# Attention block on one core: sequence-wide two-bank score tiles, fillers in a new order, middle casts on ScalarE

## The reference

```python
B, R, K, M = (16, 64, 128, 128); H, D = (8, 16); FF = 512
q = (route @ wq + bq).reshape(b_, r_, k_, H, D)      # k and v alike
scores = jnp.einsum('brkhd,brnhd->brknh', q, k) / D ** 0.5
attn = jax.nn.softmax(scores, axis=3)
out = jnp.einsum('brknh,brnhd->brkhd', attn, v).reshape(b_, r_, k_, m_)
x = _layernorm(route + (out @ wo + bo), ln1_g, ln1_b)
ff = jax.nn.relu(x @ w1 + b1) @ w2 + b2
return _layernorm(x + ff, ln2_g, ln2_b)
```

## Time and profile before

| | |
|---|---|
| median of three runs | 4756.37 us |
| the profiled execution | 4760.15 us, span 4758.1 us |
| TensorE matmul busy | 4435.0 us, 93% of the span |
| VectorE busy | 3915.0 us, 82% |
| GpSimd busy | 3623.5 us, 76% |
| ScalarE busy | 3391.7 us, 71% |
| DMA engines busy | 42.4% for the kernel's own queue |
| granted TensorE clock | 0.994 of 2.4 GHz on average |

### The profile page before, as it was taken

The page is one execution under the profiler, slowest core; times in us unless marked ns, Lnnn a source line. Parts: engine busy times, 40 slices in busy tenths (PEclk is TensorE's granted clock), DMA queues, the critical chain, the costliest instruction groups (busy, mean ns, idle before and its releaser), DMA issues.

```text
span 4758.1 us, 159188 instructions
## 1 busy us (share of the span) xinstructions
PE 4435.0 (93%) x51984; PEld 3739.4 (79%) x51984; DVE 3915.0 (82%) x11275; ACT 3391.7 (71%) x6401; POOL 3623.5 (76%) x4620
## 2 busy tenths in 40 slices
PE   5999999999999999999999999999999999999998
PEld 4787878877878877878878778878787878787886
DVE  5888888878888888888888878888888888888886
ACT  2777777767777776777777767777776777777776
POOL 4777777777777777777777777777777777777776
PEclk9999999999999999999999999999999999999999
DMA  4444444444444444444444444444444444444441
GB/s 116 115 121 119 120 120 117 122 113 119 119 120 116 122 115 122 114 121 116 123 116 121 119 116 116 123 116 121 119 121 110 123 116 121 119 121 116 120 121 53
DMA packets 756319, 556.46 MB, mean 117 GB/s; under 512 B 95872, under 2 KB 755328, under 8 KB 755456
## 3 DMA queue, kind: packets, MB, share of 16 engines
q1 hardware_dynamic: 755456, 545.81, 42.4%
HBM read 69.47 MB, written 67.11 MB: 29 GB/s over the span
## 4 chain that ended last, share of the span: by engine, by line
PE 51%; DVE 27%; issue 11%; ACT 7%; SPq 1%; DVEq 1%; ACTq 0%; POOL 0%; DMA 0%; POOLq 0%
PE bankC L629 10%; PE bankB L629 9%; DVE max_sb L535 7%; PE bankA L745 6%; PE oT_ps L645 6%; PE s_ps L662 5%; PE sT_ps L676 4%; DVE st L494 4%; PE bankB L607 4%; DVE xT_parts L559 4%; DVE ob_sb L466 4%; ACT parts L362 4%; PE bankC L601 3%; DVE onT_sb L479 3%; ACT xT_parts L407 3%
## 5 line engine op out<-in xcount | busy, mean ns | idle before, releaser
L379 ACT ACTIVATE prob_sb<-sT_ps 128x512 f32<-128x512 f32 x2048 | 1222.7, 597 | 1067.5 <-PE sT_ps L676 1067.3
L535 DVE TENSOR_REDUCE max_sb<-s_ps 128x4 f32<-128x512 f32 x2048 | 1367.6, 668 | 7.3 <-PE s_ps L662 6.1
L266 POOL TENSOR_TENSOR parts<-rest_sb,parts 128x512 bf16<-128x512 f32 x512 | 595.8, 1164 | 503.7 <-DVE parts L459 503.7
L662 PE MATMUL s_ps<-stack 96*128 96x128 bf16 x8192 | 811.7, 222 | 20.5 <-issue 14.2
L676 PE MATMUL sT_ps<-stack 99*128 99x128 bf16 x8192 | 796.9, 219 | 3.7 <-DMA stack<-max_parts 3.6
L662 PEld LDWEIGHTS s_ps<-stack 96*128 96x128 bf16 x8192 | 531.8, 98 | 339.2 <-issue 317.6
L645 PE MATMUL oT_ps<-prob_sb,v_ones 128*32 128x128 f32 x16384 | 555.1, 276 | 0.0
L676 PEld LDWEIGHTS sT_ps<-stack 99*128 99x128 bf16 x8192 | 547.8, 97 | 5.6 <-DMA stack<-max_parts 4.0
L466 DVE STREAM_TRANSPOSE ob_sb<-oT_ps 128x512 f32<-128x512 f32 x512 | 364.5, 712 | 203.5 <-PE oT_ps L645 192.7
L645 PEld LDWEIGHTS oT_ps<-prob_sb,v_ones 128*32 128x32 f32 x16384 | 417.2, 110 | 123.3 <-issue 90.6
L629 PE MATMUL bankC<-w_sb,h_sb 128*128 128x128 f32 x4096 | 513.0, 278 | 0.0
(11 more groups left out here) (80 smaller groups left out, 9256.1 us busy)
## 6 DMA issues: line engine op xcount, KB each, us to landing
stack<-parts SPq DMA_DIRECT2D x3072, 128.0 KB, 2.5
x_sb<-in_x SPq DMA_DIRECT2D x256, 256.0 KB, 3.1
out<-out_sb SPq DMA_DIRECT2D x256, 256.0 KB, 3.3
stack<-max_parts SPq DMA_DIRECT2D x768, 8.0 KB, 1.9
w_sb<-in_L_conv_w SPq DMA_DIRECT2D x2, 256.0 KB, 3.1
be_row<-in_L_conv_ln_b SPq DMA_DIRECT2D x2, 256.0 KB, 20.4
g_row<-in_L_conv_ln_g SPq DMA_DIRECT2D x2, 256.0 KB, 23.7
bo_row<-in_L_conv_bo SPq DMA_DIRECT2D x1, 256.0 KB, 8.9
```

The source lines that it names most:

```text
L266: pool.tensor_tensor(parts[:, r % 2, 3 * c + LO], rest_sb[:, c], parts[:, r % 2, 3 * c + MID], ALU.subtract).then_inc(lo_split, 1)
L379: act.activation(prob_sb[:, n % 4], sT_ps[n % 2][:], ACT.Exp, scale=float(D) ** -0.5).then_inc(exp_done, 1)
L535: dve.reduce_max(max_sb[:, (r - 2) % 2, half * HU:(half + 1) * HU, s], s_ps[n % 2][:].rearrange("p (h k) -> p h k", h=HU), AX.X).then_inc( ...
L662: ins = pe.matmul(s_ps[n % 2][:, j * P:(j + 1) * P], stack[0:PROD, (r - 2) % 4, 0, h, tok], stack[0:PROD, (r - 2) % 4, 1, h, tok], start=T ...
```

## The change

1. A step has four slots w instead of eight units. A slot scores one sequence's eight heads into one two-bank tile `s_ps` (128x1024), and the same for `sT_ps`. There is one tile of each, so a slot's scores wait for the maximum of the slot before, and its turned scores for the exponential of the slot before. VectorE takes one maximum and ScalarE one exponential of 128x1024 per slot. `prob_sb` is two buffers of eight heads (same bytes as before).
2. The fillers are in a new order. Slot 0: wo for group r-5 (it was r-4, at the end of the step), hidden chunks 2 and 3 of r-6, the transposes of x. Slot 1: both halves of `down` in a row, `attend`. Slot 2: transposes of the first norm's output, the query and the key projection. Slot 3: the transpose of the maxima (now group r-2, into `oT_ps`, not A), hidden chunks 0 and 1 of r-5, the value projection (now group r, not r-1), `attend`. The last slot scores the first sequence of group r-1, one step earlier than before.
3. The two middle casts move from VectorE to ScalarE (`mid_part`), after the last exponential of the step.
4. SyncE's order in a step is: store, load of x, the three maximum rows (of group r-2), and the 12 stack DMAs, six for the queries and then six for the keys, where each six waits for its own low part only.
5. The second normalisation is applied in two halves, one at the end of a step and one in the next; its statistics are taken in two halves beside `add_y`. ScalarE and GpSimd get one step more at the end of the program.

The diff, cut to its core:

```diff
-        s_ps = [ctx.enter_context(nc.psum_tensor(f"s_ps{b}", [P, T], F32)) for b in range(2)]
-        sT_ps = [ctx.enter_context(nc.psum_tensor(f"sT_ps{b}", [P, T], F32)) for b in range(2)]
+        s_ps, sT_ps = (ctx.enter_context(nc.psum_tensor(n, [P, H * P], F32)) for n in ("s_ps", "sT_ps"))
...
-        def sT_unit(u):
-            return (4, u + 4) if u < 4 else (3, u - 4)
+        def scored(w):
+            return (1, 0) if w == 3 else (2, w + 1)
+        def attended(w):
+            return (4, w + 2) if w < 2 else (3, w - 2)
... SyncE
+                if live(t, r, 2):
+                    sp.wait_ge(max_parts_made, upto(t, r, 2, plus=1))
+                    for part in range(MAXROWS):
+                        sp.dma_start(stack[PROD + part:PROD + part + 1, (r - 2) % 4, 0],
+                                     max_parts[:, part]).then_inc(max_rows_loaded, DMA)
                 if live(t, r, 0):
-                    sp.wait_ge(lo_split, upto(t, r, 0, per=2, plus=2))
-                    for j in range(len(Q_PARTS)):
-                        for c, part in enumerate((Q_PARTS[j], K_PARTS[j])):
+                    for c, order in enumerate((Q_PARTS, K_PARTS)):
+                        sp.wait_ge(lo_split, upto(t, r, 0, per=2, plus=c + 1))
+                        for j, part in enumerate(order):
... ScalarE
+            def mid_part(t, r, c):
+                act.wait_ge(rest_made, upto(t, r, 0, per=2, plus=c + 1))
+                act.activation(parts[:, r % 2, 3 * c + MID], rest_sb[:, c], ACT.Copy).then_inc(mid_split, 1)
...
+            def exponentials(t, r, w):
+                lag, s = attended(w)
+                if live(t, r, lag):
+                    act.wait_ge(sT_done, upto(t, r, lag, per=SEQS, plus=s + 1))
+                    if (v := upto(t, r, lag, per=2, plus=s // 2)) is not None:
+                        act.wait_ge(pv_done, v)
+                    act.activation(prob_sb[:, s % 2], sT_ps[:], ACT.Exp, scale=float(D) ** -0.5).then_inc(exp_done, 1)
... VectorE
+            def row_max(t, r, w):
+                lag, s = scored(w)
+                if live(t, r, lag):
+                    dve.wait_ge(s_done, upto(t, r, lag, per=SEQS, plus=s + 1))
+                    if (v := upto(t, r, lag, plus=-1)) is not None:
+                        dve.wait_ge(maxT_done, v)
+                    dve.reduce_max(max_sb[:, (r - lag) % 2, :, s], s_ps[:].rearrange("p (h k) -> p h k", h=H),
+                                   AX.X).then_inc(max_done, 1)
... TensorE
+            def scores(t, r, w):
+                lag, s = scored(w)
+                if live(t, r, lag):
+                    tok = slice(s * P, (s + 1) * P)
+                    if s == 0:
+                        pe.wait_ge(stack_loaded[(r - lag) % 2], upto_dma(t, r, lag, per=STACK_DMAS * DMA))
+                    if (v := upto(t, r, lag, per=SEQS, plus=s)) is not None:
+                        pe.wait_ge(max_done, v)
+                    for h in range(H):
+                        ins = pe.matmul(s_ps[:, h * P:(h + 1) * P], stack[0:PROD, (r - lag) % 4, 0, h, tok],
+                                        stack[0:PROD, (r - lag) % 4, 1, h, tok], start=True, stop=True)
+                    ins.then_inc(s_done, 1)
```

More of the change, by code:

```diff
@@ L216, in step @@
             def step(t, r):
[L218 to L222, removed]
+                if live(t, r, 7):
+                    sp.wait_ge(out_ready, upto(t, r, 7, plus=1))
+                    sp.dma_start(out_g[t + (r - 7)], out_sb[:, (r - 7) % 2]).then_inc(out_stored[(r - 7) % 2], DMA)
                 if live(t, r, -1):
@@ new lines, in scores_turned @@
+            def scores_turned(t, r, w):
+                lag, s = attended(w)
+                if live(t, r, lag):
+                    tok = slice(s * P, (s + 1) * P)
+                    if s == 0:
+                        pe.wait_ge(max_rows_loaded, upto(t, r, lag, per=MAXROWS * DMA, plus=MAXROWS * DMA))
+                    if (v := upto(t, r, lag, per=SEQS, plus=s)) is not None:
+                        pe.wait_ge(exp_done, v)
+                    for h in range(H):
+                        ins = pe.matmul(sT_ps[:, h * P:(h + 1) * P], stack[:, (r - lag) % 4, 1, h, tok],
+                                        stack[:, (r - lag) % 4, 0, h, tok], start=True, stop=True)
+                    ins.then_inc(sT_done, 1)
@@ new lines, in attend @@
+            def attend(t, r, lag, half):
+                pe.wait_ge(exp_done, upto(t, r, lag, per=SEQS, plus=2 * half + 2))
+                pe.wait_ge(v_copied, upto(t, r, lag, plus=1))
+                if (v := upto(t, r, lag, per=2, plus=half)) is not None:
+                    pe.wait_ge(oT_turned, v)
+                for k in range(2):
+                    for h in range(H):
+                        j, f = h % HU, h // HU
+                        ins = pe.matmul(oT_ps[j * VW:(j + 1) * VW, (2 * k + f) * P:(2 * k + f + 1) * P],
+                                        v_ones[:, (r - lag) % 4, 2 * half + k, h], prob_sb[:, k, h * P:(h + 1) * P],
@@ new lines, in step @@
+                scores(t, r, 0)
+                scores_turned(t, r, 0)
+                if live(t, r, 5):
+                    pe.wait_ge(onT_made, upto(t, r, 5, plus=1))
+                    pe.wait_ge(v_copied, upto(t, r, 0))
+                    for s in range(SEQS):
+                        ins = pe.matmul(A[:, s * P:(s + 1) * P], onT_sb[:, s * P:(s + 1) * P], wo_sb[:],
+                                        start=True, stop=True)
+                    ins.then_inc(wo_done, 1)
+                if live(t, r, 6):
+                    hidden(t, r, 6, 2)
+                    hidden(t, r, 6, 3)
@@ new lines, in step @@
+                if live(t, r, 0):
+                    pe.wait_ge(x_loaded[r % 2], upto_dma(t, r, 0))
+                    if (v := upto(t, r, 5, plus=1)) is not None:
+                        pe.wait_ge(z_done, v)
+                    elif (v := upto(t, r, 0)) is not None:
+                        pe.wait_ge(v_copied, v)
+                    transposes(A, [x_sb[:, r % 2, s] for s in range(SEQS)]).then_inc(xT_done, 1)
+                scores(t, r, 1)
+                scores_turned(t, r, 1)
+                if live(t, r, 6):
+                    down(t, r, 0)
+                    down(t, r, 1)
@@ new lines, in step @@
+                if live(t, r, 5):
+                    hidden(t, r, 5, 0)
+                    hidden(t, r, 5, 1)
+                if live(t, r, 0):
+                    pe.wait_ge(xT_joined, upto(t, r, 0, plus=1))
+                    pe.wait_ge(rest_made, upto(t, r, 0, per=2, plus=1))
+                    for s in range(SEQS):
+                        ins = pe.matmul(A[:, s * P:(s + 1) * P], xT_sb[:, s * P:(s + 1) * P],
+                                        wv_sb[:], start=True, stop=True)
+                    ins.then_inc(v_done, 1)
```

547 lines of the change are left out of this document (230 added, 317 removed).

## The result

The changed kernel takes 4439.53 us (median of 4 runs, 4437.33 to 4442.55); the kernel before, beside it on the same chip, 4757.39 us (4755.48 to 4759.14). The ratio is 0.9332 [0.9316, 0.9349], 6.7% faster. The sum of the prediction was 4545 us, and its range ended at 4475: the direction was right, the size was outside the range.

What follows compares the result with a forecast made beforehand. TensorE was taken as nearly the bound. A step from 18.09 to 17.25 us (17.05 work, 0.2 wait), times 251, saved 211 us: 4549 from the profiled 4760.15, 4545 as median, 8-in-10 range 4475 to 4690.

Steps and rivals of the forecast that it cites:

- wo's wait: TensorE's output projection waits for `onT_sb`, 0.99 us a step before; claimed to go once wo comes in the next step.
- The wait that was expected: Hidden chunk 1 in slot 3 waits on bank C for both `rest` operations: 0 to 0.3 us, taken as 0.2.
- the three new durations: Maximum of 128x1024 on VectorE 1.20 us, exponential of 128x1024 on ScalarE 1.02, cast on ScalarE 0.60.
- the last maximum's slack: Scores of the next slot 0 need VectorE's last maximum, done at 16.6 and wanted at 17.25: slack 0.6 us.
- SyncE's: The stack's 12 DMAs land at 28.4 and are wanted at 29.7 in slot 3: slack 1.2 us, cost nothing.
- VectorE's sum: VectorE's busy time in a step was to fall from 15.3 to 13.9 us, under 17 and not the bound.
- TensorE's work in a step: TensorE's new step without any wait, summed from the pitches of the trace before: 17.05 us.
- The sign that the prediction named: If right, wo's pitch from step to step on TensorE would be 17.2 to 17.3 us.
- The 0.15 for the values: Extra charged where the fp32 value projection precedes attention in slot 3, as `down` costs 0.15 us more there than before scores.
- No wait at all: Rival: overlaps on ScalarE and VectorE cover chunk 1's wait, a step of 17.05 us, 4495 us; chance 0.15.
- One bank set is not enough: Rival: with one tile of each kind, late handovers stall TensorE, a step of 17.75 us, 4671 us; chance 0.23.
- The stack arrives late: Rival: SyncE's issues at 0.95 us each make the step 18.45, 4846 us; chance 0.08 with another ring.

Runs made afterwards that it cites:

- the experiment with wo alone: The kernel before, with wo moved on TensorE from the end of unit 6 to behind the scores of unit 7: 4652.94 us, 0.9782.
- Half width: The changed kernel with every maximum and every exponential split into two instructions of 128x512, tiles and order unchanged: 4454.48 us, 0.9364 of the kernel before.
- the values first: The changed kernel with the value projection ahead of hidden chunk 1, and the copy of v ahead of its relu: 4365.22 us, 0.9173 of the kernel before.
- the paired version of before: The kernel before, with TensorE's units taken in pairs (scores of both, turned scores of both, fillers of both), other engines untouched: 4822.28 us, 1.0138.
- triples behind blocks: The version with the value projection ahead of chunk 1, with key product and hidden chunk 2 put directly behind bf16 score blocks: 4587.16 us, 0.9641 of the kernel before.
- the version with parted blocks: The changed kernel with wo, the transposes of x and of the maxima each between a slot's scores and turned scores: 4444.54 us, 0.9341 of the kernel before.

## Why the prediction was right and wrong

**What bounds it, and wo's wait.** Right: TensorE's order bounds before and after, and wo's wait was time that anything may fill (the experiment with wo alone).

**The wait that was expected.** Right in place and cause, 0.26 measured for 0.2. Half width, which makes the chain to the second `rest` longer, raises it to 0.32, and other work in its place (the values first) fills it.

**Durations and slack.** Right: the three new durations, the last maximum's slack, and SyncE's (another order of its DMAs changed nothing). VectorE's sum was off, without effect: 13.9 us a step was predicted, 3748.7 / 256 = 14.6 it is. The prediction took the full length of operations off a busy time in which consecutive operations overlap.

**TensorE's work in a step.** This step failed: 17.05 was taken, 16.58 it is, and 0.47 x 251 = 118 us is more than the whole miss of 105; the wait, 0.06 larger than thought, takes 15 us back, and the remaining 103 us are nearly all that lies between 4545 and 4440. The sign that the prediction named, a wo pitch of 17.2 to 17.3, did not come: it is 16.84. The prediction priced every group by one pitch of before, as if it were a property of the group. It depends on what stands beside it, and on whether the group starts behind a wait:

| | priced | measured after |
|---|---|---|
| wo, now in front of a triple and without a wait | 0.99 | 0.87 |
| transpose of the maxima, now in front of a triple | 0.12 | 0.03 |
| hidden chunk 3, key product, now behind a triple | 0.78 | 0.71, 0.69 |
| transposes of n, now without a wait | 0.42 | 0.36 |
| values in front of attention | 0.95 + 0.15 | 0.98 |

Other rows differ by 0.03 or less. Two effects are in the table.

First, the row *ahead* of a triple of fp32r products is short: wo 0.87 (0.95 in front of a block), the maxima's transpose 0.03 (0.11), the values 0.81 in the version that puts them there (0.98 in front of attention). A bf16 block ahead of a triple gives only 0.03 (0.42 for 0.45). Behind another triple it shows in that one's place: 0.69 and 0.71 in front of scores and transposes. In front of attention it doesn't: the one triple of before that stands directly behind another costs 0.78 there, like the first, so the trace of before had no row with the low price.

```profile
2399.54 0.95 PE L607 MATMUL bankA<-xT_parts,wk_parts 128*128 128x512 f32 x3
2400.32 0.85 PE L607 MATMUL bankC<-nT_parts,w_parts 128*128 128x512 f32 x3
2401.10 1.08 PE L645 MATMUL oT_ps<-prob_sb,v_ones 128*32 128x128 f32 x32
```

Two triples put behind blocks cost 0.13 in one version and 0.17 in the other, so 0.07 to 0.09 each.

Second, wo and the transposes of n stood behind waits in before, which added 0.04 (0.99 against 0.95) and 0.06 (0.42 against 0.36) to their own pitches. So about 0.1 of the 0.30 went with the waits, and about 0.2 is neighbours. That is 0.05 for each of the four triples, less than the 0.07 to 0.09, as chunk 1 and the values became 0.02 and 0.03 dearer in their new places.

The 0.15 for the values was carried over from `down`, a group of another shape; 0.03 of it was there.

**The chances.** Faster had 0.90. "No wait at all" gave 4495 from the same floor; with the floor at 16.58 even the forecast with its wait lies below it, so the low end of the range held no case in which the floor itself was wrong. Its mechanism was not the one: there is a wait. "One bank set is not enough" doesn't decide here, where the maxima held TensorE up 7 times, 5.9 us in all; a wait for the maxima does decide in the paired version of before, and in that with triples behind blocks, 0.73 a step. "The stack arrives late" did not happen at a step of 16.84 (0.7 us of such waits from 600 to 4200 us); at 16.48 it begins to show.

**The sum, with what each part is worth in a plain step:** wo's wait -0.99, the wait behind the values -0.22, TensorE's own work -0.30 (neighbours about 0.2, starts behind waits about 0.1), the new wait +0.26.

The Trainium skill (Perfetto Trace Analysis, Optimizing Scalar/DVE Operations), which the prediction weighed on the casts, holds for the engine's own time, 0.621 against 0.409; the same sentence there leaves room for the move where VectorE is saturated. The kernel lost 64 us when they went back, with VectorE 85% busy in the changed kernel and on TensorE's path.

Open: why a triple costs more behind bf16 matmuls, and why attention behind it takes the gain away. No run here separates its weight loads from its matmuls. That the effect exists is shown by the rows and by the versions that part blocks; how the 0.30 divides is a sum of pitches, each good to 0.01 or 0.02.

## What to carry to other kernels

When a reordered engine is the bound, price each group by rows that have the same neighbours and no wait ahead of them, and give the range a case in which the floor without waits is off by some per cent: here 0.3 of 16.9 us, in every step, was 75 us, enough to move the result out of the range. After a change, look at TensorE's pitches, and at the waits of the weight loads as well as those of the matmuls, for what still waits, and put there an operation whose inputs come earlier. Here a single PSUM tile of each kind cost next to nothing (5.9 us in all) as long as the fillers between two writes lasted longer than its reader took to come and read; with one product between them it cost 0.73 us a step.

## What was not expected of the hardware

- The pitch of a group depends on its neighbours: an fp32r triple of 512 columns takes 0.78 us, and right behind another one 0.69 to 0.71 in front of scores or transposes, but 0.78 in front of attention; wo, eight matmul records of fp32, takes 0.87 in front of a triple and 0.95 in front of bf16 scores; the transpose of the maxima 0.03 or 0.11.
- A group that starts behind a wait costs more itself: wo 0.99 or 1.00 instead of 0.95, the transposes of n 0.42 instead of 0.36.
- A jump of the hardware loop costs 5.6 to 6.7 us in the changed kernel, 4.7 to 6.3 in the version with parted blocks, and 6.7 to 7.8 in the one with the values first, each with a body of 48 steps; with a body of 120 the one jump costs 4.8. Four jumps became one for 27 us.
